# A two-layer vision tower on one core: third patch tile in float32, FFN weight passes in quarters, last products in other PSUM banks

## The reference, cut to what matters

```
h  = concat(cls, patches @ W.T + b) + pos_enc                      # tok
x  = layernorm(h)                                                  # n0
u  = layernorm(x) * gamma + beta
z, c = sigmoid(u @ Wg.T + bg), u @ Wc.T + bc
h  = h + scan(state = (1 - z) * state + z * c) + x                 # gate, scan, h1
g  = gelu(layernorm(h) @ ternary(W_fc).T)                          # fc
h  = h + (layernorm(g) * ln_w + ln_b) @ ternary(W_proj).T          # gw, tg, proj
h  = h + softmax(causal(rope(q) @ rope(k).T / 16)) @ v @ Wf.T + bf # qk, score, attend
h  = h + (clip(round(layernorm(h) / scale), -127, 127) * scale) @ (ternary_weight - 1).T + bias   # n3, clip, round, out
```

## Time and profile before

| what | us |
|---|---|
| runs of the kernel before | 156.7, 156.85, 157.93 |
| their median | 156.85 |
| the profiled execution, its own time | 157.96 |
| its span, first to last instruction | 155.9 |
| mean granted TensorE clock in it | 0.977 |
| busy: TensorE, VectorE, ScalarE, GpSimd | 146.1, 129.8, 104.0, 87.6 |

### The profile page before, as it was taken

One profiled execution on the slowest core, in us unless ns is written; L12 is line 12 of the kernel. 1 busy time (PEld: TensorE's weight loads), 2 busy tenths in 40 slices (PEclk: granted clock), 3 DMA queues, 4 the chain that ended last, 5 costly groups with the idle time before them and its releaser, 6 DMA issues.

```text
span 155.9 us, 3371 instructions
## 1 busy us (share of the span) xinstructions
PE 146.1 (94%) x1003; PEld 128.1 (82%) x1003; DVE 129.8 (83%) x395; ACT 104.0 (67%) x254; POOL 87.6 (56%) x139
## 2 busy tenths in 40 slices
PE   7997989998999998999999999999999999999751
PEld 7987979897888886788889988989899989877540
DVE  1275888689999999989999786998878898999951
ACT  3345999423873599999897987943992354788540
POOL 1019739987760322872458817396940978846520
PEclk9999999999999999999999999999999999999955
DMA  5999996003000003500000000000000000012241
GB/s 167 310 404 400 415 395 240 3 4 115 22 0 0 4 0 90 225 2 6 0 2 2 8 2 0 4 4 2 2 2 0 6 0 0 6 31 58 58 117 49
DMA packets 5728, 12.31 MB, mean 79 GB/s; under 512 B 1120, under 2 KB 3024, under 8 KB 5328
## 3 DMA queue, kind: packets, MB, share of 16 engines
q1 hardware_dynamic: 5712, 12.11, 22.0%
HBM read 10.82 MB, written 1.21 MB: 77 GB/s over the span
## 4 chain that ended last, share of the span: by engine, by line
PE 59%; DVE 18%; issue 6%; POOL 6%; DMA 4%; SPq 3%; ACT 1%; DVEq 0%; POOLq 0%
PE bank L481 36%; PE bank L635 5%; POOL x_lo L1338 5%; DMA x_raw<-x_in 4%; SPq L424 3%; PE bank L714 3%; PE bank L575 3%; PE bank L699 3%; DVE stats L970 3%; DVE hs L1153 2%; POOL small L1314 2%; DVE residual L1289 2%; PE bank L559 2%; DVE zc L1143 2%; DVE hs L1169 2%
## 5 line engine op out<-in xcount | busy, mean ns | idle before, releaser
L1314 POOL TENSOR_TENSOR small<-small,powers 119x1 f32<-119x1 f32 (+3 forms) x51 | 36.8, 724 | 40.4 <-DVE small L982 27.2
L1338 POOL TENSOR_TENSOR x_lo<-x_raw,x_hi 128x714 fp32r<-128x714 f32 x8 | 14.6, 1831 | 11.6 <-ACT x_hi L788 11.6
L481 PE MATMUL bank<-pj,gt_hi 128*119 128x256 f32 x80 | 20.1, 290 | 0.0
L481 PE MATMUL bank<-pj,gt_lo 128*119 128x256 f32 x80 | 19.4, 281 | 0.0
L888 ACT ACTIVATE gt_hi<-bank 128x476 fp32r<-128x476 f32 x20 | 11.1, 570 | 7.1 <-PE bank L635 7.0
L1379 POOL TENSOR_TENSOR qk<-rope 128x476 f32<-128x476 f32 (+1 forms) x12 | 12.2, 1039 | 5.8 <-DVE rope L1241 5.8
L481 PE MATMUL bank<-fc,n1t_hi 128*119 128x512 f16 x40 | 15.2, 379 | 0.0
L481 PE MATMUL bank<-fc,n1t_lo 128*119 128x512 f16 x40 | 15.1, 378 | 0.0
L559 PE MATMUL bank<-wt_hi,x_hi 128*119 128x256 f32 x48 | 13.9, 289 | 1.4 <-ACT x_hi L788 0.8
L481 PEld LDWEIGHTS bank<-pj,gt_lo 128*119 128x119 f32 x80 | 14.5, 181 | 0.0
L481 PEld LDWEIGHTS bank<-pj,gt_hi 128*119 128x119 f32 x80 | 14.4, 181 | 0.0
(11 more groups left out here) (172 smaller groups left out, 465.7 us busy)
## 6 DMA issues: line engine op xcount, KB each, us to landing
x_raw<-x_in SPq DMA_DIRECT2D x10, 357.0 KB, 8.7
turns<-turns_in SPq DMA_DIRECT2D x1, 1190.0 KB, 5.7
w_fc<-w_fc_in SPq DMA_DIRECT2D x1, 1024.0 KB, 7.7
w_pj<-w_pj_in SPq DMA_DIRECT2D x1, 1024.0 KB, 11.4
out_dram<-residual SPq DMA_DIRECT2D x10, 96.0 KB, 1.7
w_tok<-w_tok_in SPq DMA_DIRECT2D x2, 384.0 KB, 4.7
w_gate<-w_gate_in SPq DMA_DIRECT2D x1, 512.0 KB, 8.9
w_qk<-w_qk_in SPq DMA_DIRECT2D x1, 512.0 KB, 14.8
```

The source lines that it names most:

```text
L481: last = mm(out, a, b, start=(n == 0), stop=(n == len(pairs) - 1))
L1314: return gt(small[0:held(i, r), i, r:r + n], small[0:held(i, r), i, mv + 1:mv + 2 * n:2], powers[0:held(i, r), 0:n], ALU.pow)
L1338: gt(x_lo[:, i, :, 0:n], x_raw[:, i, :, 0:n], x_hi[:, i % X_SLOTS, :, 0:n].bitcast(F32), ALU.subtract).then_inc(s["x_lo_ready"], 1)
```

## The change

`FULL_TILES` goes from 2 to 3, so tile 2 is multiplied as float32 and `split:2` is gone from ScalarE and GpSimd. `w_below` and `w_ternary` on VectorE are eight stages each in place of two, a quarter of a matrix (128 x 512) at a time; all that waits for a finished matrix waits for four pieces. `out` takes its banks from the wide ring, 5 to 7, and its first product is issued ahead of the wait for `q3t`. The four lists are ordered anew throughout; the stages in them are otherwise the same.

```diff
-FULL_TILES = 2
+FULL_TILES = 3
+PIECES = 4
 RINGS = {
...
-    "narrow": ((0, 1), ("gate_bias", "fold", "value_bias", "abs_sum", "ln_bias", "hs", "proj", "value", "score", "attend",
-                        "out")),
+    "narrow": ((0, 1), ("gate_bias", "fold", "value_bias", "abs_sum", "ln_bias", "hs", "proj", "value", "score", "attend")),
-    "wide": ((5, 6, 7), ("gate", "fc", "qk")),
+    "wide": ((5, 6, 7), ("gate", "fc", "qk", "out")),
...
-                pe.wait_ge(s["pj_ready"], 1)
+                pe.wait_ge(s["pj_ready"], PIECES)
...
             def out_(i):
                 n = seen_rows(i)
                 out = claim(("out", i))
+                if i == 0:
+                    pe.wait_ge(s["out_rows_ready"], 2)
+                mm(out[0:n, 0:D], pick[0:STACK, 0:n], out_rows[0:STACK, :], start=True, stop=False)
                 pe.wait_ge(s["q3t_ready"], i + 1)
                 if i == 0:
                     pe.wait_ge(s["w_out_ready"], 1)
-                    pe.wait_ge(s["out_rows_ready"], 2)
-                mm(out[0:n, 0:D], pick[0:STACK, 0:n], out_rows[0:STACK, :], start=True, stop=False)
...
+            def piece(w, q):
+                k = w.shape[1]
+                if k >= PIECES:
+                    return slice(k // PIECES * q, k // PIECES * (q + 1)), slice(0, w.shape[2])
+                per, width = PIECES // k, w.shape[2] * k // PIECES
+                return slice(q // per, q // per + 1), slice(q % per * width, (q % per + 1) * width)
-            def w_below(n):
+            def w_below(u):
+                n, q = divmod(u, PIECES)
                 out, w, _ = ternary[n]
+                ks, cols = piece(w, q)
                 dve.wait_ge(s["cut_ready"], 2)
-                ts(out[:, :, :], w[:, :, :], derived[:, D_NEG_CUT + n:D_NEG_CUT + n + 1], None, ALU.is_lt)\
+                ts(out[:, ks, cols], w[:, ks, cols], derived[:, D_NEG_CUT + n:D_NEG_CUT + n + 1], None, ALU.is_lt)\
                     .then_inc(s["below_ready"], 1)
```

More of the change, by code:

```diff
@@ L121 @@
     "tensor": """
[L122 to L131, removed]
@@ L172 @@
[L172 to L178 removed]
+        warm:0 tok:0 tok:1 seat:0 seat:1 tok:2 seat:2 tok:3 t0:0 seat:3 t0:1 w_gate:0 t0:2 tok:4 t0:3 seat:4
@@ new lines @@
+        w_ternary:0 tok:5 t0:4 seat:5 tok:6 tok:7 seat:6 tok:8 seat:7 seat:8 tok:9 t0:5 seat:9 w_fold:0 t0:6
+        w_fold:1 t0:7 gate:0 gate:1 w_value_bias:0 gate:2 gate:3 w_ln_bias:0 gate:4 gate:5 h1:0 h1:1 gate:6 t0:8
+        h1:2 h1:3 t0:9 gate:7 t1:0 gate:8 gate:9 t1:1 gate:10 fc:0 fc:1 t1:2 gate:11 h1:4 h1:5 fc:2 fc:3 h1:6
+        fc:4 t1:3 tg:0 h1:7 fc:5 fc:6 tg:1 fc:7 t1:4 tg:2 proj:0 tg:3 t1:5 fc:8 fc:9 tg:4 proj:1 tg:5 t1:6 fc:10
+        tg:6 fc:11 tg:7 proj:2 t1:7 h1:8 fc:12 fc:13 tg:8 h1:9 tg:9 proj:3 tg:10 fc:14 t2:0 proj:4 tg:11 value:0
@@ new lines @@
+        t1:8 fc:15 t2:1 t2:2 proj:5 fc:16 t2:3 fc:17 tg:12 tg:13 qk:0 value:1 qk:1 tg:14 proj:6 t1:9 tg:15 qk:2
+        tg:16 qk:3 t2:4 tg:17 proj:7 value:2 fc:18 t2:5 fc:19 score:0 t2:6 score:1 proj:8 t2:7 tg:18 score:2
+        score:3 tg:19 qk:4 qk:5 turn:0 proj:9 qk:6 attend:0 qk:7 turn:1 t2:8 value:3 value:4 attend:1 turn:2
+        t2:9 value:5 attend:2 turn:3 qk:8 attend:3 score:4 qk:9 value:6 score:5 qk:10 score:6 qk:11 turn:4
+        value:7 attend:4 turn:5 t3:0 score:7 turn:6 attend:5 value:8 score:8 out:0 score:9 turn:7 attend:6 t3:1
@@ new lines @@
+        attend:7 turn:8 t3:2 score:10 out:1 out:2 t3:3 attend:8 value:9 out:3 turn:9 t3:4 attend:9 t3:5 value:10
+        turn:10 out:4 out:5 attend:10 t3:6 out:6 t3:7 out:7 t3:8 out:8 t3:9 out:9 t3:10 out:10""",
+    "scalar": """
+        w_tok:0 w_tok:1 split:3 w_abs_fc:0 split:4 n0:0 t0:0 w_gate:0 t0:1 split:5 t0:2 n0:1 w_abs_pj:0 split:6
+        split:7 t0:3 n0:2 split:8 n0:3 split:9 n0:4 t0:4 n0:5 w_qk:0 t0:5 n0:6 n0:7 t0:6 w_fold:0 t0:7 n0:8
+        w_fold:1 n0:9 gate:0 gate:1 gate:2 gate:3 t0:8 t0:9 n1:0 n1:1 t1:0 gate:4 gate:5 n1:2 t1:1 fc:0 t1:2
+        fc:1 n1:3 square:0 fc:2 fc:3 t1:3 fc:4 tg:0 n1:4 fc:5 tg:1 square:1 t1:4 n1:5 fc:6 fc:7 tg:2 tg:3
+        square:2 t1:5 fc:8 n1:6 tg:4 fc:9 tg:5 t1:6 square:3 tg:6 tg:7 n1:7 square:4 fc:10 fc:11 fc:12 t1:7 n2:0
+        square:5 tg:8 tg:9 n2:1 tg:10 t2:0 fc:13 n1:8 n2:2 tg:11 fc:14 t1:8 t2:1 t2:2 n2:3 fc:15 square:6 fc:16
+        t2:3 tg:12 value:0 square:7 tg:13 fc:17 square:8 tg:14 n1:9 t1:9 value:1 tg:15 n2:4 tg:16 n2:5 t2:4
+        tg:17 n2:6 value:2 fc:18 t2:5 fc:19 t2:6 n2:7 score:0 t2:7 tg:18 square:9 tg:19 score:1 n2:8 turn:0
+        score:2 score:3 turn:1 t2:8 value:3 n2:9 value:4 turn:2 t2:9 value:5 turn:3 n3:0 n3:1 value:6 score:4
+        score:5 left_value:0 turn:4 value:7 score:6 turn:5 turn:6 n3:2 t3:0 score:7 value:8 n3:3 turn:7 score:8
+        t3:1 n3:4 turn:8 t3:2 t3:3 n3:5 score:9 value:9 turn:9 t3:4 score:10 n3:6 n3:7 t3:5 value:10 turn:10
+        n3:8 t3:6 t3:7 n3:9 t3:8 n3:10 t3:9 t3:10""",
```

92 lines of the change are left out of this document (40 added, 52 removed).

## The result

The changed kernel took 159.9 us (median of six runs, 158.26 to 160.03); the kernel before, run beside it, 156.77 (six runs, 156.55 to 157.93). The ratio is 1.0149, with a 95% interval from 1.0107 to 1.0191: slower by 1.5%, 2.3 us. The prediction said 156.1, with a range to 157.7. The sign was wrong and the time lies outside the range. The profiled executions stand 2.0 us apart (159.96 and 157.96), their spans 2.2 (158.1 and 155.9).

What follows compares the result with a forecast made beforehand. VectorE was taken to bound the kernel before 60 us, TensorE the middle, and the last seven microseconds to have their own bound; + 0.5 early, - 1.0 and - 0.2 at the end, off 156.85, gave 156.1 us, range 154.6 to 157.7.

Steps and rivals of the forecast that it cites:

- `n0:5` 0.2 us late: Ahead of VectorE's full stretch: `w_below` quarters meeting GpSimd's low halves were to delay `n0:5` by 0.2 us.
- the bound of 1.2: Latest case given for `n0:5`: 1.2 us late, with one quarter per low half; the earliest was 0.7 early.
- rival A: VectorE and GpSimd alternate strictly at shared SBUF access, one quarter per low half; early + 1.5, 157.15 us; chance 0.14.
- slower by more: Whole kernel slower by more than about 1%, needing + 1.6 us from a convoy going on past tile 9; chance 0.07.
- the evidence against strict turns: At 43.37 VectorE seemed to start another two-input pass though a GpSimd copy had waited since 41.42, so may keep the turn.
- The ternary quarters: `w_ternary` quarters in VectorE's full stretch: 0.44 us more a pass, 0.88 for two, by the `wg_lo` row.
- small gaps: VectorE's idle gaps in its full stretch, 0.37 us in all, were to take up about 0.2 us.
- The clause about tile 2: Tile 2 in float32 ends 1.1 us early, but the `w_pj` load leaves 0.1 us of gain, between 0 and 0.6.
- The last products: Closing tiles: first `out` product ahead of the `q3t` wait gains 1.0 us, three banks another 0.2 before that.
- Rival C: Closing gain hidden because `n3:10` and `round:10` set the end: - 0.3 in place of - 1.2, 157.05 us; chance 0.18.
- Rival B: Quarters relieve GpSimd, `n0:5` at 31.2, ternary quarters cost half; early - 0.7, end - 1.2, 154.95 us; chance 0.23.
- the 2.68 us power: GpSimd power started at 33.85 beside a two-input pass, 2.68 us for a 0.69 us job; rival B needs it shorter.

Runs made afterwards that it cites:

- quarters_only: The kernel before with both kinds of weight pass in quarters, in the old lists; 160.26 us, ratio 1.0203.
- quarters_alone: The kernel before with only `w_below` in quarters and GpSimd's low halves of tiles 6, 7 and 8 left out; 154.82 us, one run.
- ternary_quarters: The kernel before with `w_ternary` alone in quarters, `w_below` whole; 158.36 us, ratio 1.0059.
- the pair of runs without quarters: The changed kernel with whole passes, ratio 1.0022, and the same with tile 5's low half held until `wg_lo` is done, ratio 0.9925.
- end and tile: The kernel before with the edits of the last products and tile 2 in float32, passes whole, old lists; 156.09 us, ratio 0.9913.

## Why the prediction was wrong

**What bounds the kernel: right for the kernel before.** VectorE sets the time to `h1:4`, TensorE from there; the early delay reached the end whole, less what the closing stretch gained. In the changed kernel VectorE no longer fills its stretch: it waits for TensorE for 1.06 us of it.

**The step that failed: `n0:5` 0.2 us late.** It was 2.18 late (31.91 to 34.09), beyond even the bound of 1.2. Quarters alone, without the meeting at `wg_lo`, make 2.0 of it (quarters_only, 13.92 us from `wg_lo` to `n0:5` in place of 11.91). The prediction had named the mechanism, and its price, and set it aside as rival A with 0.14, and for "slower by more" it left 0.07. Two readings led there.

First, the evidence against strict turns. The row was read rightly: the two-input pass at 43.37 does follow another while a GpSimd copy waits. But it was one copy beside two whole passes, and it was taken to hold for one-input quarters beside low halves, where quarters_only and quarters_alone show the turn passing each time. The rows for whole passes couldn't show how often turns change there, since there were hardly more passes than low halves.

Second, quarters were costed by GpSimd's delay ("eight quarters of about 0.27 us hold it up for 2.2 us") and not by VectorE's own. When turns alternate, the engine with more and shorter instructions loses a whole instruction of the other for each of its own. Three of the four quarters each last until a low half ends, and the fourth then runs freely: in quarters_only the low halves end at 29.63 us and the quarters at 30.30, after 5.42 us; alone they take 1.67. From this follows `mean0:5` at 31.3 in place of 27.35. The prediction saw `n0:5` wait for GpSimd and took GpSimd's queue as the cause; it didn't ask what VectorE owes to GpSimd first.

Rival A's walk had the picture right: it put `h0:5` at 31.0 (31.66 in the changed kernel, 31.04 in quarters_only) and `n0:5` at 33.1 (34.09 and 33.93), too early, since the `pj` quarters met more than it had counted (2.81 us in quarters_only, 1.62 alone). Its early + 1.5 was + 3.57. The Trainium skill names the contention (GPSIMD Engine Reference, section Specifications), as the prediction quoted. The runs agree that it is there (1.67 us alone, 5.44 beside low halves) and add what that sentence leaves open: one-input quarters lose the turn to each low half that waits, while the copy at 41.42 is passed over once.

**The ternary quarters: + 0.88, less 0.32 for `t0:3` and 0.2 for small gaps; measured + 1.39.** From `n0:5` to `h1:4` it is 29.82 us after (63.91 - 34.09) and 28.43 before (60.34 - 31.91). The price was right: 0.93 us by the rows of the changed kernel, 0.38 a pass in ternary_quarters (2.68 - 2.30), 0.44 predicted, 0.13 us for each further piece. The 60 ns of the Trainium skill (VectorE: DVE Perf Modes, TRN2 errata) would be 0.18 a pass by an estimate and is too low here; the same section says that its table under-predicts and gives about 150 cycles as measured, which would be 0.47 by an estimate from it. The step that failed is the 0.2 us that gaps were to take up. VectorE's idle time grew instead, by 0.87 us, with 1.06 of waiting for TensorE in it: the late tiles left TensorE busy for 0.26 of the 2 us before 40 us, its clock was at about half from 40 to 44, and it came late in its turn. The - 0.32 for `t0:3` did leave the stretch, but ahead of `n0:5` there was no idle time left to take it.

ternary_quarters has nearly the same length (29.84 us) by another way: there the second pass meets the output-bias rows (+ 0.6), which it doesn't in the changed kernel, and VectorE waits no longer than before. That the two agree is chance.

**The clause about tile 2: right in size, incomplete.** Tile 2 starts at 11.98 us and takes 2.75, near the 11.65 and 2.53 worked, and early nothing came of it (60.42). Not costed was that the new ScalarE list puts `split:5` right behind `t0:1`, ahead of `t0:2` and `n0:1`: GpSimd can start the low half at 19.95 in place of 21.28, and it falls on `wg_lo`. The prediction looked at `wg_lo` as a price for quarters and never asked what would run beside it. By the pair of runs without quarters this is 0.6 to 1.0%; in the changed kernel itself it isn't separated from the quarters, which delay the same `n0:5`.

**The last products: right.** - 1.0 - 0.2 predicted, 0.78% of 157 us = 1.2 measured; in the changed kernel, 94.19 against 95.56 from `h1:4` on. The closing walk in the changed kernel, from `n3:10` to the last drain:

```profile
152.13 0.60 ACT L797 ACTIVATE s<-residual,small 80x256 f32<-80x256 f32 x1 [0.22 <-POOL small L1415]
```

```profile
155.03 0.48 DVE L1303 SCALAR_TENSOR_TENSOR residual<-bank,derived,residual 80x256 f32<-80x256 f32 x1 [0.69 <-PE bank L738]
```

is 3.38 us; 52.3 - 49.1 = 3.2 had been walked. Rival C falls with it. Rival B falls too: its "for", the 2.68 us power that has to shrink, was right (1.08), and nobody was waiting for it.

**The sum as the runs give it**, in per cent of the kernel before: end and tile - 0.9, one-input quarters + 1.15, ternary quarters + 0.6, `wg_lo` + 0.5 to 1.0. That makes + 1.4 to + 1.9, and 1.5 was measured. The agreement is in part luck, as the 0.6 of the ternary quarters holds a meeting that the changed kernel doesn't have, and lacks its waits for TensorE. Together the two kinds of quarters cost more than apart (2.03 against 1.74, within the intervals).

## What to carry to other kernels

Before a pass is cut into pieces, list what the other engine of the shared access runs in that stretch, and cost each piece at one whole instruction of the other (here 1.8 us for a piece of 0.4), and not at its own length; cutting helped only the other engine here, the one with the fewer, longer instructions. A reordering that only moves an instruction on a third engine can make two others meet, so after moving a step look at what then runs beside it, and not only at what it waits for. And idle time that another step will fill isn't there to be spent twice.
